# Expert blocks over chosen rows only, with the state space layer of one half of the tokens beneath the expert blocks of the other

## The chip, the cores and the metric

The program runs on one core of a Trainium2 chip. The metric is the device time of one execution in microseconds, the median of several runs. TensorE (PE in the profile) multiplies, VectorE (DVE) and ScalarE (ACT) work elementwise and read PSUM, GpSimd (POOL) works on SBUF only, and the queue of SyncE (SP) starts the transfers between memory and SBUF.

## What is computed

2048 tokens (8 sequences of 256) of width 256, all in float32, go through four layers, each added to its input and then normalised:

```python
x = layernorm(x + attention(x))      # 16 heads of 128, causal
x = layernorm(x + moe0(x))           # 32 experts of width 96, the 6 best of each token, plus a shared one of 192
x = layernorm(x + state_space(x))    # in-projection, 4-tap convolution, 8 heads, gate, out-projection
x = layernorm(x + moe1(x))           # 16 experts of width 176, the 4 best of each token, plus a shared one of 352
```

An expert is `silu(x @ gate) * (x @ up) @ down`, weighted per token by the router's normalised score; the weight of an expert that a token did not choose is zero.

## The kernel before

**Attention.** Eight groups of two heads (`group`) run over 16 units each (two heads by eight sequences). Each product of two float32 matrices is done as three passes over rounded halves (`hi` and `lo`, type float32r; helper `passes`, issued by `chain` at L352). Beside it ACT and POOL split the weights of the later layers into such halves, 56 items of 128x768 (`split_high` L650, `split_low` L544), and SP stores them to memory.

**Expert layers.** They are dense: every token goes through every expert. The hidden units of all experts and of the shared one are cut into tiles of 128. A step `s` is one hidden tile for one quarter (quad) of the tokens, 512 of them. `gate_up(s)` multiplies with the gate and the up weights: 2 outputs by 2 chunks by 3 passes, 12 matmuls of 512 columns. ACT takes the silu (`gate`, L742), DVE the product (`activate`, L1082), POOL multiplies with the router's weights, which a transfer has spread over the partitions (`combine`, L578), ACT and DVE round the result into halves (`high`, L750; `low_half`, L1088), and `down(s)`, two steps later, adds it to the output of the quad: 4 token tiles by 3 passes, 12 matmuls of 256 columns. There are 204 steps (4 quads by 26 tiles for the first expert layer, 4 by 25 for the second).

**State space layer.** A pair is 512 tokens (two sequences). The work of pair `p` is written out by hand beneath the steps, at offsets from `FRONT = 33, 65, 97, 129`: ten in-projections (`project`), the convolution (`conv_start`, `taps`, `conv_silu`), a scan of decays over 128x768 for each head (`decays` L1152), its product with the Gram matrix on POOL (`mixes` L600), the head's product on PE (`products`), outputs (`outputs` L1160 and L1163), the out-projection (`project_out`), and `out_add` L1181. `ln_stats`, `ln_root` and `ln_rows` (L920 to L934) normalise a quad.

The order on each engine is the order in which the program issues. An engine never goes past an instruction that waits. SP also waits in its order, for buffers that come free. After the last step DVE adds the last quad (`add_down`), normalises it and SP stores it (L488).

Of the kernel before, what the change touches and what calls it, by code (L numbers as in the profile page):

```python
# [7 lines left out]
I32 = mybir.dt.int32  # L8
# [32 lines left out]
L0 = dict(layer=0, experts=32, width=96, shared=192, top=6, rows=32, reuse=3)  # L41
L1 = dict(layer=1, experts=16, width=176, shared=352, top=4, groups=4, top_groups=2, rows=16, reuse=11)
LAYERS = L0, L1
for _l in LAYERS:
    _l["lead"] = -(-_l["shared"] // P)
    _l["tiles"] = _l["lead"] + _l["experts"] * _l["width"] // P
    _l["combs"] = _l["experts"] * _l["rows"] // P
# [8 lines left out]

IN_JOBS = 10
PART = 256
IN_ITEM = L0["tiles"]
L1_ITEM = IN_ITEM + -(-IN_JOBS // 3)  # L60
SPLITS = 8
ITEMS = SPLITS * (GROUPS - 1)
assert L1_ITEM + L1["tiles"] <= ITEMS

STEPS = QUADS * (L0["tiles"] + L1["tiles"])
LAG = 2
HALF = P // 2


def step(s):  # L70

    n = QUADS * L0["tiles"]
    if s < n:
        return L0, s // L0["tiles"], s % L0["tiles"]
    return L1, (s - n) // L1["tiles"], (s - n) % L1["tiles"]


def first_step(f, q):
    return f["layer"] * QUADS * L0["tiles"] + q * f["tiles"]


def shared(s):
    f, _, j = step(s)
    return j < f["lead"]


def packed(s):

    f, _, j = step(s)
    return f["shared"] % P == HALF and j == f["shared"] // P  # L90


def ups(s):

    return sum(not packed(i) for i in range(s + 1))


def rows_of(s):

    return slice(HALF, P) if packed(s) else slice(0, P)  # L100


def combed(s):

    return sum(not shared(i) for i in range(s + 1))


def comb_blocks():

    for f in LAYERS:  # L110
        for q in range(QUADS):
            for m in range(f["combs"]):
                s0 = first_step(f, q) + f["lead"] + m * f["reuse"]
                yield f, q, m, s0, s0 + f["reuse"] - 1


COMBS = list(comb_blocks())


def comb_block(s):  # L120
    f, q, j = step(s)
    return f["layer"] * QUADS * L0["combs"] + q * f["combs"] + (j - f["lead"]) // f["reuse"]


def comb_landed(k):

    return sum(16 * (P // COMBS[i][0]["rows"]) for i in range(k % 2, k + 1, 2))


FRONT = 33, 65, 97, 129  # L130
NORM0 = None, 1, 10, 19
NORM1 = 28, 54, 82, 115


def program(nc, x_rows, x_cols, attn_w, l0_gate, l1_gate, w_all, ssm_cols, out_w, out):
    with ExitStack() as ctx:
# [36 lines left out]
        causal_at = keep.at  # L173
        causal = keep("causal", [P, 2 * P])
        x = keep("x", [P, TILES, D])
        xT_hi = keep("xT_hi", [P, DC, T], F32R)
        xT_lo = keep("xT_lo", [P, DC, T], F32R)
# [60 lines left out]
        def unit(u):  # L238
# [3 lines left out]


        TOP = 34 * 1024
        top_at = (nc.sbuf_usable_end - TOP) // 64 * 64
        assert r.at <= top_at
        low = Region(keep.at)
        gated, act_sb = low("gated", [P, 2, BANK]), low("act_sb", [P, 2, BANK])
        act_hi, act_lo = low("act_hi", [P, 2, BANK], F32R), low("act_lo", [P, 2, BANK], F32R)

        stage = Region(top_at)
        raw_stage = stage("raw_stage", [P, 2, 3 * PART])
        split_stage = stage("split_stage", [P, 2, 3, 2, PART], F32R)
        high = Region(top_at)
        GU_RING, D_RING = 3, 3
        gu_w = high("gu_w", [P, GU_RING, 2, 2, PART], F32R)
        d_w = high("d_w", [P, D_RING, 2, PART], F32R)
        high.at = max(high.at, stage.at)
        comb = high("comb", [P, 2, BANK])
        gate_w = [{n: high(f"l{i}_gate_{n}", [P, DC * f["experts"]], dt) for n, dt in (("raw", F32), ("hi", F32R), ("lo", F32R))}  # L260
                  for i, f in enumerate(LAYERS)]
        logit, score, weight, comb_tok = (high(n, [P, QUAD, 32]) for n in ("logit", "score", "weight", "comb_tok"))
        choices = [high(f"l{i}_choice", [P, QUAD, f["experts"] + 8]) for i, f in enumerate(LAYERS)]
        chosen = high("chosen", [P, QUAD, SEL])
        top8, group_top8 = high("top8", [P, QUAD, 8]), high("group_top8", [P, QUAD, 8])
        group_choice, group_chosen = high("group_choice", [P, QUAD, 16]), high("group_chosen", [P, QUAD, 16])
        row_stat = high("row_stat", [P, QUAD])
        combT, logitT = high("combT", [32, BANK]), high("logitT", [32, BANK])

        small = Region(causal_at)  # L270
        cols = small("cols", [P, CJ * (TAPS + 1) + 2 * EJ + 2])
        ones_col, a_col = small("ones_col", [P, 1]), small("a_col", [P, 1])
        dt_tok = small("dt_tok", [P, 4, NH])
        mean_sq, rms, rms_tmp = (small(n, [P, 4]) for n in ("mean_sq", "rms", "rms_tmp"))

        IN_RING, DECAY_RING, MIXES = 3, 2, 3
        in_w = low("in_w", [P, IN_RING, 2, PART], F32R)
        mix_hi, mix_lo = low("mix_hi", [P, 2, SEQ], F32R), low("mix_lo", [P, 2, SEQ], F32R)
# [1434 lines left out]
```

## Time and profile before

| | |
|---|---|
| median of 3 runs | 1664.05 us (1663.39 to 1666.93) |
| span of the profiled execution | 1664.1 us |
| busy PE / DVE / ACT / POOL | 1607.4 / 1131.1 / 764.6 / 628.7 us |
| moved by transfers | 277.75 MB |

The profiled execution's own time and its span are the same to 0.1 us, and both are those of the median. Busy times are sums over one engine's instructions. The duration of a matmul in the trace overlaps the one before it, so that a PE that is always busy need not be at its peak: the rate is read from the distance between the starts of neighbours.

### The profile page before, as it was taken

Reading aid. Unit: us, or ns where it says so; the run is one execution under the profiler, and the core shown is the slowest. Engines: PE = TensorE matmul, PEld = TensorE weight load, DVE = VectorE, ACT = ScalarE, POOL = GpSimd, SP = SyncE. Lnnn points to the kernel's source line nnn. Section 1 sums busy time; section 2 is a strip of 40 time slices with the busy share of each in tenths; the row PEclk is TensorE's granted clock in tenths of the full one; section 3 lists DMA queues with packets and bytes.
Section 4 is the critical chain, followed back from the end, with each engine's and each line's share of the span. In section 5 each row is a group of like instructions: output and inputs, shape, how many; then the busy total and the mean of one; then the engine's idle time right before and its main releaser. Section 6 shows DMA issues by size and latency. Waiting matters only on the chain.

```text
span 1664.1 us, 29632 instructions
## 1 busy us (share of the span) xinstructions
PE 1607.4 (97%) x9944; PEld 1403.7 (84%) x9944; DVE 1131.1 (68%) x2877; ACT 764.6 (46%) x1889; POOL 628.7 (38%) x379
## 2 busy tenths in 40 slices
PE   7999999999999979999999999999999999999997
PEld 6988888898888868888888888888888888888886
DVE  5878878787887765556467568748784867753533
ACT  5666656666665543434433443325333533323221
POOL 2322223232222004323377335841575147533242
PEclk9999999999999999999999999999999999999999
DMA  6444335343443016666676556655655466555563
GB/s 212 159 140 143 141 118 180 132 158 139 142 141 137 1 59 205 191 196 205 199 225 188 184 176 209 194 187 165 207 189 175 146 206 197 178 175 172 195 206 107
DMA packets 101241, 277.75 MB, mean 167 GB/s; under 512 B 13488, under 2 KB 17584, under 8 KB 100112
## 3 DMA queue, kind: packets, MB, share of 16 engines
q1 hardware_dynamic: 101136, 276.39, 51.6%
q8 instruction: 61, 1.00, 0.2%
q14 instruction: 44, 0.36, 0.1%
HBM read 229.18 MB, written 46.63 MB: 166 GB/s over the span
## 4 chain that ended last, share of the span: by engine, by line
PE 60%; issue 14%; DVE 13%; POOL 6%; ACT 4%; DMA 1%; SPq 1%; POOLq 0%; DVEq 0%; ACTq 0%
PE psum L352 54%; POOL act_sb L578 4%; PE psum L1324 2%; DVE s_sb L1019 1%; PE psum L1335 1%; PE psum L1514 1%; POOL mix L600 1%; ACT p_sb L701 1%; PE psum L1314 1%; ACT kT_hi L660 1%; DVE s_sb L1017 1%; DVE kT_lo L913 1%; DVE pT_lo L1034 1%; DVE x L934 1%; DVE p_sb L1027 1%
## 5 line engine op out<-in xcount | busy, mean ns | idle before, releaser
L352 PE MATMUL psum<-xT_hi,gu_w 128*128 128x512 f32 x1616 | 550.3, 401 | 4.2 <-DVE act_sb L1082 4.0
L578 POOL TENSOR_TENSOR act_sb<-act_sb,comb 128x512 f32<-128x512 f32 x184 | 311.1, 1691 | 614.8 <-DVE act_sb L1082 614.6
L1082 DVE TENSOR_TENSOR act_sb<-psum,gated 128x512 f32<-128x512 f32 x204 | 140.7, 690 | 378.9 <-PE psum L352 372.6
L742 ACT ACTIVATE gated<-psum 128x512 f32<-128x512 f32 x204 | 122.2, 599 | 600.3 <-PE psum L352 597.8
L352 PEld LDWEIGHTS psum<-xT_hi,gu_w 128*128 128x128 f32 x1616 | 304.2, 188 | 78.0 <-DVE act_sb L1082 5.6
L352 PE MATMUL psum<-xT_lo,gu_w 128*128 128x512 f32 x808 | 319.6, 395 | 0.0
L352 PEld LDWEIGHTS psum<-d_w,act_hi 128*128 128x128 f32 x1632 | 221.5, 188 | 19.7 <-issue 2.1
L544 POOL TENSOR_TENSOR split_stage<-raw_stage,split_stage 128x768 fp32r<-128x768 f32 x56 | 103.1, 1840 | 354.2 <-ACT split_stage L650 354.2
L352 PE MATMUL psum<-d_w,act_hi 128*128 128x256 f32 x1632 | 227.7, 282 | 0.4 <-ACT act_hi L750 0.4
L352 PEld LDWEIGHTS psum<-xT_lo,gu_w 128*128 128x128 f32 x808 | 152.2, 188 | 28.8
L1088 DVE TENSOR_TENSOR act_lo<-act_sb,act_hi 128x512 fp32r<-128x512 f32 x204 | 148.8, 729 | 2.1 <-ACT act_hi L750 1.8
L750 ACT ACTIVATE act_hi<-act_sb 128x512 fp32r<-128x512 f32 x204 | 127.3, 624 | 17.1 <-POOL act_sb L578 16.9
L699 ACT ACTIVATE p_sb<-s_sb,neg_max 128x128 f32<-128x128 f32 x128 | 51.5, 403 | 172.0 <-DVE neg_max L1019 172.0
L352 PE MATMUL psum<-d_w,act_lo 128*128 128x256 f32 x816 | 130.1, 282 | 0.0
L352 PE MATMUL psum<-xT_hi,aw_hi 128*128 128x512 f32 x256 | 104.1, 407 | 9.9 <-POOL aw_lo L540 9.9
L352 PEld LDWEIGHTS psum<-d_w,act_lo 128*128 128x128 f32 x816 | 111.2, 188 | 0.0
L352 PE MATMUL psum<-xT_hi,aw_lo 128*128 128x512 f32 x256 | 102.1, 399 | 0.0
L352 PE MATMUL psum<-xT_lo,aw_hi 128*128 128x512 f32 x256 | 101.8, 398 | 0.0
L600 POOL TENSOR_TENSOR mix<-mix,gram 128x768 f32<-128x768 f32 x32 | 94.3, 2947 | 0.0
L1026 DVE TENSOR_SCALAR p_sb<-p_sb,row_inv 128x128 f32<-128x128 f32 x128 | 83.1, 649 | 4.6
L352 PE MATMUL psum<-aw_hi,xT_hi 128*128 128x256 f32 x256 | 74.7, 292 | 9.7 <-DVE kT_lo L913 8.3
L352 PE MATMUL psum<-aw_hi,zT_hi 128*128 128x256 f32 x256 | 80.5, 315 | 2.5 <-DVE zT_lo L1039 2.5
(203 smaller groups left out, 3473.6 us busy)
## 6 DMA issues: line engine op xcount, KB each, us to landing
gu_w<-w_split SPq DMA_DIRECT2D x204, 512.0 KB, 3.6
d_w<-w_split SPq DMA_DIRECT2D x204, 256.0 KB, 3.8
w_split<-split_stage SPq DMA_DIRECT2D x56, 768.0 KB, 3.9
raw_stage<-w_all SPq DMA_DIRECT2D x56, 384.0 KB, 4.3
decay_all<-decay_dram SPq DMA_DIRECT2D x32, 384.0 KB, 5.3
in_w<-w_split SPq DMA_DIRECT2D x40, 256.0 KB, 4.1
aw_raw<-attn_w SPq DMA_DIRECT2D x8, 1024.0 KB, 6.3
comb<-l_comb_dram SPq DMA_DIRECT2D x128, 64.0 KB, 3.1
```

Of the source, the lines that this page charges most:

```text
L352: last = nc.tensor.matmul(out_ap, w, m, start=start and n == 0, stop=stop and n == len(pairs) - 1, **kw)
L544: pool.tensor_tensor(split_stage[:, k % 2, :, 1, :], raw_stage[:, k % 2, :].rearrange("p (j w) -> p j w", j=3), split_stage[:, k % 2, :, 0 ...
L578: pool.tensor_tensor(act_sb[:, s % 2, :], act_sb[:, s % 2, :], comb[:, comb_block(s) % 2, :], ALU.mult).then_inc(comb_done, 1)
L600: pool.tensor_tensor(mix[:, g % MIXES], mix[:, g % MIXES], gram[:], ALU.mult).then_inc(mix_ready, 1)
L660: act.activation(kT_hi[:, bp % 2, j // 2, :], bank, ACT.Copy).then_inc(qkv_hi, 1)
L699: act.activation(p_sb[:, u % 3, 0:P], s_sb[:, u % 2, 0:P], ACT.Exp, bias=neg_max[:, u % 3, 0:1], scale=-1.0, accum_out=row_sum[:, u % 3, 0:1])
L742: act.activation(gated[to, s % 2, :], psum[0:to.stop - to.start, G_BANK, :], ACT.Silu).then_inc(gated_ready, 1)
L750: act.activation(act_hi[rows_of(s), s % 2, :], act_sb[rows_of(s), s % 2, :], ACT.Copy).then_inc(act_hi_ready, 1)
L1026: dve.tensor_scalar(p_sb[:, u % 3, 0:P], p_sb[:, u % 3, 0:P], row_inv[:, u % 3, 0:1], None, ALU.mult)
L1082: dve.tensor_tensor(act_sb[r, s % 2, :], psum[r, G_BANK if packed(s) else U_BANK, :], gated[r, s % 2, :], ALU.mult).then_inc(t_ready, 1)
L1088: dve.tensor_tensor(act_lo[r, s % 2, :], act_sb[r, s % 2, :], act_hi[r, s % 2, :].bitcast(F32), ALU.subtract).then_inc(act_lo_ready, 1)
L1324: last = pe.transpose(psum[:, PT_BANK, i * P:(i + 1) * P], p_sb[:, u % 3, i * P:(i + 1) * P], ident[:])
```

## The change

**Expert layers.** The router's choice is turned into row numbers. For each half of the tokens (1024) every expert gets a region of 1024 rows in a scratch array `xs` in memory; `rank` counts on PE, with a triangular matrix, the place of each token in each chosen expert's region, `slots` turns it into row numbers, and POOL scatters each token row there (`scatter`: one indirect transfer of 128 rows of 1 KB per token tile and choice). `table` works out which regions hold how many blocks of 128 rows. The stream of blocks is then of fixed length: per half 79 blocks in the first expert layer and 47 in the second, which is enough for any choice; what is left over works on rows of zeros. For each block SP reads the expert's number and row into registers, loads its weights (128x640 float32 in the first layer, 128x1280 in the second) and its rows (`block_load`), PE turns the rows, multiplies gate, up and down in plain float32 without halves, ACT copies and takes the silu, DVE multiplies, and SP stores two blocks of output at once (`block_store`). For each token tile POOL gathers the 6 or 4 output rows of each token back (`gather`, one indirect transfer for each choice), and DVE adds them with their weights (`combine`). The shared experts are 32 more blocks in each layer, with weights that stay in SBUF. `xs` is zeroed in memory during the attention, 77 MB in 42 transfers from SP, in place of the splitting of weights.

**Order.** Stream: 32 shared blocks of layer 0; 79 blocks of its half 0; 79 of its half 1; 16 shared and 47 of layer 1, half 0; 16 shared and 47 of layer 1, half 1. The combining of layer 0, the state space layer and the routing of layer 1 for half 0 are placed in 90 slots beneath the 79 blocks of layer 0, half 1; those of half 1 in 90 slots beneath the 63 blocks of layer 1, half 0. The state space layer multiplies in plain float32 as well, with in-projection weights that stay in SBUF, and the roundings into halves go. The attention's own code is the same, but three quads instead of one are normalised and two routed in its last group.

The core of the diff:

```diff
+HALVES = 2
+BLOCK = 128
+STREAM = shared_blocks(L0, range(TILES))
+FIRST = {}
+for _f, _h in ((L0, 0), (L0, 1), (L1, 0), (L1, 1)):
+    if _f is L1:
+        FIRST["shared", _h] = len(STREAM)
+        STREAM += shared_blocks(L1, range(HALF_TILES * _h, HALF_TILES * (_h + 1)))
+    FIRST[_f["layer"], _h] = len(STREAM)
+    STREAM += routed_blocks(_f, _h)
+FRONT = 8, 40
+SLOTS = 90
+SPAN = (FIRST[0, 1], FIRST["shared", 0]), (FIRST["shared", 0], FIRST["shared", 1])
+def mix_slot(j):
+    return 1 + j if j < QUAD else 16 + 4 * (j - QUAD)
+def gather_slot(j):
+    return max(0, mix_slot(j) - (1 if j < QUAD else 3))
...
+            def scatter(f, q):
+                if f["layer"] == 0 and q == 0:
+                    pool.wait_ge(xs_zeroed, 16 * ZEROED * (GROUPS - 1))
+                pool.wait_ge(placed, QUADS * f["layer"] + q + 1)
+                for t in range(QUAD * q, QUAD * (q + 1)):
+                    for k in range(f["top"]):
+                        pool.indirect_dma_start(xs[q // 2], bass.IndirectOffsetOnAxis(ap=row_of[:, t, k:k + 1], axis=0), x[:, t, :], None) \
+                            .then_inc(scattered[q], 16)
...
+                for k in range(f["top"]):
+                    pool.indirect_dma_start(og[:, i % MIX_RING, k, :], None, os[f["layer"]][t // HALF_TILES],
+                                            bass.IndirectOffsetOnAxis(ap=back_of[f["layer"]][:, t, k:k + 1], axis=0)).then_inc(og_loaded[i % MIX_RING], 16)
...
+            def block_gate_up(n):
+                for i in range(3 if f["layer"] else 2):
+                    at = i * h.stop
+                    last = chain(psum[h, gu_bank(n), i * P:(i + 1) * P], [(w[:, c * f["up"] + at:c * f["up"] + at + h.stop], rows[c]) for c in range(DC)])
+                last.then_inc(gu_ready, 1)
+            for n in range(BLOCKS):
+                if n + 2 < BLOCKS and is_routed(n + 2):
+                    block_turn(n + 2)
+                if n + 1 < BLOCKS:
+                    block_gate_up(n + 1)
+                block_down(n)
...
+            def combine(f, t):
+                dve.wait_ge(b_copied, OUTPUTS[SHARED_AT[f["layer"], t] + SHARED])
+                chained(dve.tensor_tensor(x[:, t, :], x[:, t, :], acc[:, t, :], ALU.add))
+                dve.wait_ge(og_loaded[i % MIX_RING], 16 * gathered(f, t))
+                for k in range(f["top"]):
+                    ins = dve.scalar_tensor_tensor(x[:, t, :], og[:, i % MIX_RING, k, :], mix_of[f["layer"]][:, t, k:k + 1], x[:, t, :], ALU.mult, ALU.add)
...
             def project(p, k):
-                n, part = IN_JOBS * p + k, slice(p * PT, (p + 1) * PT)
-                pe.wait_ge(in_loaded[n % IN_RING], 16 * (n // IN_RING) + 16)
-                pairs = []
-                for c in range(DC):
-                    w = slice(c * P, (c + 1) * P)
-                    pairs += passes(in_w[:, n % IN_RING, 0, w], in_w[:, n % IN_RING, 1, w], xT_hi[:, c, part], xT_lo[:, c, part])
-                chain(psum[:, proj_bank(k), :], pairs).then_inc(proj_ready, 1)
+                part = slice(p * PT, (p + 1) * PT)
+                chain(psum[:, proj_bank(k), :], [(in_w[:, k, c, :], xT[:, c, part]) for c in range(DC)]).then_inc(proj_ready, 1)
...
+                        if o == 48:
+                            scatter(L1, p)
...
+            all_stored(L1, 1)
+            for t in range(HALF_TILES, TILES):
+                gather(L1, t)
```

## Rows read from the trace of the kernel before

**Rows 1.** The page, busy us (share) xinstructions; and the group that counts the steps

```profile
PE 1607.4 (97%) x9944; PEld 1403.7 (84%) x9944; DVE 1131.1 (68%) x2877; ACT 764.6 (46%) x1889; POOL 628.7 (38%) x379
L1082 DVE TENSOR_TENSOR act_sb<-psum,gated 128x512 f32<-128x512 f32 x204 | 140.7, 690 | 378.9 <-PE psum L352 372.6
```

**Rows 2.** Windows: attention, expert steps, tail (PE, PEld, DVE, ACT, POOL, clock, DMA)

```profile
0.00:611.00 611.00, 571.63 (x3990) 517.53 (x3991) 479.51 (x1586) 378.84 (x1251) 146.44 (x103) 1.00 0.38 132
611.00:1654.00 1043.00, 1035.75 (x5956) 886.17 (x5954) 645.40 (x1266) 385.80 (x638) 482.30 (x276) 1.00 0.60 188
1654.00:1664.00 10.00, 0.00 (x0) 0.00 (x0) 6.19 (x26) 0.00 (x0) 0.00 (x0) 0.70 0.15 52
```

**Rows 3.** Timeline of PE, float32r matmuls of one expert step

```profile
830.46 0.63 PE L352 MATMUL psum<-xT_hi,gu_w 128*128 128x512 f32 x2
830.93 0.39 PE L352 MATMUL psum<-xT_lo,gu_w 128*128 128x512 f32 x1
...
831.39 1.11 PE L352 MATMUL psum<-d_w,act_hi 128*128 128x256 f32 x8
832.33 0.64 PE L352 MATMUL psum<-d_w,act_lo 128*128 128x256 f32 x4
832.80 0.39 PE L352 MATMUL psum<-xT_hi,gu_w 128*128 128x512 f32 x1
```

**Rows 4.** Timeline of PE, plain float32: transposes, then matmuls of 256, 256, 128, 128

```profile
823.50 0.60 PE L1495 MATMUL psum<-ident,conv 128*128 128x128 f32 x4
823.86 0.48 PE L352 MATMUL psum<-xT_hi,gu_w 128*128 128x512 f32 x1
```

```profile
803.77 0.92 PE L1484 MATMUL psum<-later,conv 64*128 64x256 f32 x4
804.62 0.50 PE L352 MATMUL psum<-xT_hi,gu_w 128*128 128x512 f32 x1
```

**Rows 5.** Groups of DVE and ACT by form: busy us, mean ns of one

```profile
L1152 DVE TENSOR_TENSOR_SCAN mix<-decay_all,start_row 128x768 f32<-128x768 f32 x32 | 82.5, 2579 | 0.1
L1181 DVE SCALAR_TENSOR_TENSOR x<-psum,rms,x 128x256 f32<-128x256 f32 x16 | 7.0, 476 | 0.0
L1143 DVE TENSOR_TENSOR h_tok<-psum,dt_tok 128x512 f32<-128x512 f32 x16 | 10.9, 682 | 0.0
L713 ACT ACTIVATE zT_hi<-psum 128x256 fp32r<-128x256 f32 x128 | 49.7, 388 | 2.2 <-PE psum L1335 1.4
L708 ACT ACTIVATE pT_last<-psum 128x128 f32<-128x128 f32 x128 | 33.9, 265 | 3.5 <-PE psum L1324 3.5
```

**Rows 6.** POOL's products and SP's issue of a transfer: ns min/median/max, or mean

```profile
L600 POOL TENSOR_TENSOR mix<-mix,gram x32: 1832/3294/3307, 834.0 to 1433.3; 128x768 f32<-128x768 f32 x32
L484 SPq DMA_DIRECT2D decay_all<-decay_dram x32: 377/431/674, 809.5 to 1412.8; - x32
```

```profile
L578 POOL TENSOR_TENSOR act_sb<-act_sb,comb 128x512 f32<-128x512 f32 x184 | 311.1, 1691 | 614.8 <-DVE act_sb L1082 614.6
```

**Rows 7.** Attention: one DVE line (ns min/median/max), then waits (us, times, longest)

```profile
L1026 DVE TENSOR_SCALAR p_sb<-p_sb,row_inv x128: 285/289/1561, 28.3 to 601.4; 128x128 f32<-128x128 f32 x128
```

```profile
PE psum L1324 <- DVE pT_lo L1034: 14.0, 18, 2.4
PE psum L352 <- DVE kT_lo L913: 8.3, 9, 2.0
```

**Rows 8.** Timeline of DVE and SP after the last matmul

```profile
1653.77 1.29 DVE L1095 TENSOR_TENSOR x<-psum,x 128x512 f32<-128x512 f32 x2 [1.12 <-PE psum L352]
...
1659.33 1.38 DVE L934 TENSOR_SCALAR x<-x,mv,rstd 128x256 f32<-128x256 f32 x4
```

```profile
1660.74 0.39 SPq L488 DMA_DIRECT2D out<-x  x1
```

More of the change, by code:

```diff
@@ L57 @@
 IN_JOBS = 10
[L58 to L84, printed above, removed]
@@ L87, in packed @@
[L87 to L114, printed above, removed]
@@ L117, with shared_blocks @@
[L117 to L135, printed above, removed]
+def shared_blocks(f, tiles):
+    return [(f, None, t, s) for t in tiles for s in range(SHARED)]
@@ new lines, with is_routed, gives_output @@
+SHARED_AT = {(f["layer"], t): n for n, (f, h, t, s) in enumerate(STREAM) if h is None and s == 0}
+def is_routed(n):
+    return STREAM[n][1] is not None
+def gives_output(n):
+    return is_routed(n) or STREAM[n][3] == SHARED - 1
+ROUTED = [n for n in range(BLOCKS) if is_routed(n)]
+ROUTED_OF = {n: r for r, n in enumerate(ROUTED)}
+OUTPUTS = [0]
+for _n in range(BLOCKS):
+    OUTPUTS.append(OUTPUTS[-1] + gives_output(_n))
+L0_ROUTED = HALVES * L0["blocks"]
+XB_RING, OUT_RING = 4, 4
+L1_RING = 4
@@ new lines, with out_place, ring_of, gathered @@
+L0_RING = 2 * L1_RING
+def out_place(n):
+    f, h, m, _ = STREAM[n]
+    before = sum(-(-STREAM[FIRST[k]][0]["blocks"] // 2) for k in ((0, 0), (0, 1), (1, 0), (1, 1)) if FIRST[k] < FIRST[f["layer"], h])
+    return before + m // 2, m % 2
+def ring_of(r):
+    if r < L0_ROUTED:
+        return r % L0_RING, r // L0_RING
+    r -= L0_ROUTED
+    k = r % L1_RING
+    return k, len(range(k, L0_ROUTED, L0_RING)) + r // L1_RING
+def gathered(f, t):
+    return sum(LAYERS[i]["top"] for i in range(2) for u in range(TILES)
+               if (i, u) <= (f["layer"], t) and (i * TILES + u) % 2 == (f["layer"] * TILES + t) % 2)
@@ L271, in program @@
[L271 to L278, printed above, removed]
-        square, square_sum = low("square", [P, PT]), low("square_sum", [P, PT])
@@ new lines, in _, with first_row_of @@
+            rows_of = {}
+            def first_row_of(n):
+                f, h, m, _ = STREAM[n]
+                if m % 8 == 0:
+                    if m == 0:
+                        sp.wait_ge(rows_known, HALVES * f["layer"] + h + 1)
+                    _, rows_of[f["layer"], h] = nc.values_load_multi_w_load_instructions(
+                        rows_at[f["layer"]][h][0:1, m:m + 8], engines=[mybir.EngineType.SP], min_val=0, max_val=f["last_row"],
+                        skip_runtime_bounds_check_because="a sum over all experts of rows that exist, whoever chose what")
+                return rows_of[f["layer"], h][m % 8]
@@ L521, in _ @@
                         store(q)
-            store(QUADS - 1)
+            for q in range(2, QUADS):
+                store(q)
             sp.wait_ge(stored, 16 * QUADS)
@@ new lines, in weights @@
+                of = by_expert(place, f)[:, tiles, :]
+                chained(dve.scalar_tensor_tensor(of, of, 1.0, shift[:, h, 0:e].rearrange("p (a e) -> p a e", a=1).to_broadcast([P, QUAD, e]),
+                                                 ALU.add, ALU.add))
+                chained(dve.tensor_tensor(of, of, by_expert(mask, f)[:, tiles, :], ALU.mult))
+                for i in range(QUAD):
+                    last = dve.max(places[:, QUAD * q + i, :], of[:, i, :])
+                chained(last)
```

1405 lines of the change are left out of this document (707 added, 698 removed).

## Prediction

> **What bounds the kernel now.** I read the page first, then windows by stage, then PE's timeline inside an expert step, then the groups of the other engines, and the end. The page gives PE 97% of the span [rows 1]. The windows cut this into attention to 611 us, 204 expert steps from 611 to 1654, and a tail of 10 us [rows 2]. In the expert stage PE is busy 1035.75 of 1043 us at full clock, DVE 645, POOL 482, ACT 386, with the transfer engines at 0.60 [rows 2]. PE's order alone sets this stage: 5.1 us a step. Inside it the starts give the rates. Two float32r matmuls of 512 columns take 0.47 us (0.235 each), twelve of 256 columns 1.41 us (0.118 each) [rows 3]. A step is 12 of each, 4.23 us, so 863 us for 204; the other 180 us are the state space layer and the normalisations beneath. The reader should see that the change must be judged on PE first, and then on whoever becomes late once PE is relieved.
>
> **Prices on PE in plain float32.** A plain float32 product shows in the trace as two instructions. The four of L1484 (256, 256, 128 and 128 columns) take 0.85 us to the next start [rows 4]. Two passes over 768 columns at the rate of [rows 3] would be 0.71; four would be 1.41 and one 0.35, so it is two an instruction, and the 0.14 left goes with the change to another type. So I take 0.235 us per instruction of 256 columns and 0.118 per one of 128: four times the float32r price per column, against three passes before. A transpose of 128 costs 0.09 [rows 4], taken as 0.10. A block of layer 0 is then 2 transposes (0.20), 4 products of 128 columns (0.94) and one of 256 (0.47): 1.61 us. A block of layer 1 is 0.20 + 6 x 0.235 + 2 x 0.47 = 2.55 us. Shared blocks have no transposes: 1.41 and 2.35 us.
>
> The sum of the blocks on PE: 158 x 1.61 = 254, 94 x 2.55 = 240, 32 x 1.41 = 45, 32 x 2.35 = 75, together 614 us for 863: 249 us less. The state space layer gets dearer. For each of four pairs: 10 in-projections of 2 x 0.94 (was 6 x 0.235), 18.8 us; 8 heads of 1.41, 11.3 us; 16 out-products of 0.47, 7.5 us; turns, Gram products and routing about 6. That is 43.6 a pair, 87 for a half.
>
> **Stage by stage**, with what else binds there.
>
> *Attention, 605 us (was 611).* The 56 splits go from ACT and POOL. They also held up DVE: L1026 takes 289 ns in the median and up to 1561 [rows 7]. But PE waits for DVE here only 22 us in all [rows 7], and the last group gets two more normalisations and one more routing on DVE, about 15 us of which half shows. Bounds 595 to 620.
>
> *32 shared blocks, 60 us.* PE 45 plus 5 for turns and routing. DVE has about 28 us of routing and normalising among the first 12 blocks, where PE has 22, so 10 us are lost.
>
> *79 blocks of layer 0, half 0, 155 us.* PE needs 127. Each block moves 328 KB of weights, 131 KB of rows in and 131 KB out, 46.6 MB in all, and 48 scatters add 6.3 MB. The window of the expert stage moves 188 GB/s at a share of 0.60 [rows 2], which would be 313 GB/s when full: 169 us. Short packets may cost more, long ones less; at 370 GB/s it is 143. I take 155: transfers bind here for the first time.
>
> *POOL's indirect transfers.* There are 96 + 64 scatters and as many gathers, 320 in all. The trace of before has none. Nearest rows: SP's issue of a transfer, 0.43 us, and a POOL product of 128x512, 1.69 us [rows 6]. I take 1.0 us, about the middle, and keep 0.43 and 1.7. The trace shows no transfer started by POOL. The Trainium skill (DMA: Bandwidth & Descriptors, "Latency and other measured facts") gives about 1 us to the first byte of a transfer that GpSimd prepares; by it the sum would be the same, and no run here shows it yet.
>
> *79 blocks of layer 0, half 1, over the state space layer of half 0, 269 us.* PE 127 + 87 + 2 = 216. DVE: 79 products (0.27, as ACT's 128x128 from PSUM [rows 5]) 21; 8 combines of 7 chained operations of 256 columns, 0.48 each [rows 5], 28; four normalisations of a quad, 5.6 each (first to last row of the tail, less the add [rows 8]), 22; state space 90, of it 16 scans of 2.58 [rows 5]; routing and out_add 29. That is 190 in 216. ACT: 79 x (0.39 + 0.27 + 0.39) = 83 [rows 5], plus 66. So no engine is over PE in sum, but PE, DVE and POOL wait for each other in order. (1) At the start, slots 0 to 3 gather four tiles: 4 for the stores to land, 24 on POOL, 2 to land, 3.5 for the last combine, against 5.6 us in which PE reaches slot 4 and 3 of slack: 25 lost. DVE stands at the combine, block products are queued behind it, and PE waits for them. (2) In slots 13 to 28 POOL has four gathers (24) and eight products of 2.95 (23.6; mean of 3.29 and less [rows 6]) in 42 us of PE: 5. (3) At slot 56 the 16 scatters of pair 0 (16 us) stand before the products of pair 1, which have 5 to 8 us of lead: 11. (4) DVE's bursts, a normalisation or a routing of 5 us, against a lead of about 4 us: 12. Sum 269.
>
> *63 blocks of layer 1, half 0, over half 1, 296 us.* PE 38 + 120 + 87 = 245. The start is worse, since the scatters of pair 1 were issued two slots before the end: 31. Then 3, 9 and 8 for the other three.
>
> *63 blocks of layer 1, half 1, 175 us.* PE 158. The 47 routed ones move 43 MB and the gathers 4 MB, at 313 to 370 GB/s 150 to 127 us, after 38 us of shared blocks that move little: 165 to 188. I take 175, with transfers as the bound again.
>
> *Tail, 49 us (was 10).* After the last store (3), 32 gathers at 1.0, 2.5 to land, a last combine 2.5, one normalisation 5.6, the store 3.3 (1660.74 to the end [rows 8]). Nothing covers this.
>
> Sum: 605 + 60 + 155 + 269 + 296 + 175 + 49 = 1609, say **1610 us**. The sum stands against the profiled execution's 1664.1 us, which is the median of the runs: 3.3% faster. PE's own need from the first block to the last falls from 1036 us to 50 + 127 + 216 + 245 + 158 = 796, so 240 us are gained there and 199 given back: 160 as waits, 104 of them in the two overlapped stages, and 39 in the tail.
>
> **Rivals.**
>
> *A. The waits are hidden, PE sets the end.* For it: DVE has 190 of 216 us, and before PE lost only 7 of 1043 us to anyone [rows 2] with a DVE at 62%. Against it: blocks are three times shorter than steps, so the same burst is no longer covered. With indirect transfers at 0.5 us and half of my waits: 600 + 52 + 143 + 235 + 262 + 162 + 35 = 1490 us.
>
> *B. POOL is slower: the kernel ends slower.* Place: the gathers at the start of both overlapped stages, the scatters at slot 56, the tail. My sum holds 150 exposed indirect transfers (24 + 40 + 2 x 16 + 32, and some 20 at slots 13 to 28). Each 0.1 us more costs 15 us, so above 1.36 us the change loses. A POOL product rises from 1.83 to 3.29 us when DVE scans beside it [rows 6]. If the transfers cost as L578's product, 1.69, the sum is 1610 + 104 = 1714 us. The Trainium skill (SBUF - State Buffer, "Who interferes with whom") says that GpSimd and a DVE operation with two SBUF inputs or a two-port mode take one port in turn, and that descriptors wait for it as well; L600's two durations agree. That rule speaks against this change, and this is its rival.
>
> *C. Transfers bind.* Rows of 1 KB are new to this trace. At 250 GB/s half 0 of layer 0 takes 53 MB / 0.25 = 212 us and the last stage 38 + 188 = 226, the two between keep 252 and 240 under what they need anyway: 1610 + 57 + 51 = 1718 us. For it: 0.6 busy already at 188 GB/s [rows 2]. Against: nearly every packet before was 2 KB or more and so are the weights.
>
> *D. The hand-over inside a block binds:* PE to ACT to DVE to PE for 128 columns, 0.27 + 0.27 and two semaphores, under 1.16 us of PE. If 0.3 us of it shows in each of 316 blocks, plus 95: 1705 us.
>
> **Chances.** Forecast (1560 to 1655) 0.37; A 0.24; B 0.24; C 0.06; D 0.06; in between and within 0.2% of before 0.03. 0.2% (3 us) is about what a measurement of this kernel can tell from no change. Forecast and A are faster, 0.61; B, C and D are slower, 0.36. The range 1490 to 1720 leaves out the far halves of A and B. The likeliest case's own range is 1560 to 1655.
>
> **What would show it.** Right: PE's starts 0.118 us apart in blocks; DMA share near 1 from 665 to 820 us; DVE idle before `combine` for POOL or its transfers at the start of both overlapped stages; POOL idle little in slots 13 to 28; 40 us without a matmul at the end. Wrong: an indirect transfer of 0.5 or of 1.7 us on POOL; PE idle in small pieces in every block (D); PE idle for weights or rows (C).

## The result, and the profile after

The changed kernel takes **1994.5 us** (1992.6 to 1995.9, four runs) against 1663.8 us: 1.198 times as long (95% interval 1.196 to 1.199). Forecast was 1610, with 1490 to 1720 as the range: wrong in size and in sign.

Timed again unchanged, on three further occasions, it took 1847.7, 1844.7 and 1992.3 us, while the kernel before, run beside it each time, stayed at 1664.9 to 1665.7. So it has **two levels**, about 1846 and 1993, one per occasion: none of its 16 executions lay between, and one chip showed both (the high one with the changed kernel, the low one at another time with two close variants). I call them the low and the high level. The first profile is of the high one. The error has two parts that must be kept apart: 236 us that are always there, and 147 that come with the high level.

The page after, answering to [rows 1]: busy times, then PE, POOL and PE's granted clock in 40 slices of 50 us.

```profile
PE 1511.0 (76%) x9344; PEld 1256.6 (63%) x9344; DVE 975.6 (49%) x3299; ACT 759.6 (38%) x2327; POOL 442.1 (22%) x422
...
PE   7999999999973418788457977827898787877760
...
POOL 1010100000006470000515134261511503122015
PEclk9999999999986658799779988868998897888885
```

PE is no longer the bound (97% before). Where POOL's slice is high, PE's is low: 600 to 750, 950 to 1000, 1300 to 1350 us. The windows by stage, for [rows 2]: attention, the shared blocks as far as they are held up (614 to 754 us), the rest of them, 79 blocks of layer 0 half 0, 79 over the state space layer of half 0, 63 of layer 1 over half 1, the last 63, the tail. Columns: PE, PEld, DVE, ACT, POOL, clock, DMA share, GB/s.

```profile
0.00:614.00 614.00, 576.31 (x4018) 527.34 (x4019) 444.06 (x1654) 335.05 (x1193) 53.52 (x60) 0.98 0.42 155
614.00:754.00 140.00, 35.28 (x186) 31.27 (x184) 20.63 (x110) 8.95 (x25) 85.36 (x95) 0.57 0.29 98
754.00:787.00 33.00, 32.07 (x223) 29.40 (x224) 9.21 (x37) 13.78 (x38) 0.00 (x0) 0.90 0.06 18
787.00:956.00 169.00, 136.69 (x945) 117.15 (x944) 44.49 (x163) 77.55 (x237) 0.00 (x0) 0.94 0.84 269
956.00:1286.00 330.00, 237.24 (x1366) 188.19 (x1366) 157.64 (x435) 127.48 (x310) 109.95 (x89) 0.86 0.59 183
1286.00:1666.00 380.00, 290.62 (x1521) 212.03 (x1521) 184.90 (x495) 123.75 (x301) 119.04 (x103) 0.86 0.50 160
1666.00:1934.00 268.00, 202.75 (x1092) 151.20 (x1091) 85.74 (x321) 72.95 (x227) 42.89 (x45) 0.87 0.59 188
1934.00:1994.00 60.00, 0.00 (x0) 0.00 (x0) 28.88 (x87) 0.09 (x1) 31.32 (x32) 0.51 0.30 90
```

From 614 to 754 us PE works 35 of 140 us, DVE 21 and ACT 9. The groups of the operations that I had to price, for [rows 5, 6]:

```profile
L633 POOL DMA_INDIRECT og<-l_os,l_back_of x160 | 161.4, 1009 | 575.0 <-DMA l_os<-b_out 310.1
...
L618 POOL DMA_INDIRECT xs<-x,row_of x160 | 159.9, 1000 | 236.3 <-DVE row_of L1026 189.4
```

The timelines of ACT and of SP in the stop. In brackets: the idle time before, and what ended it.

```profile
690.49 0.27 ACT L790 ACTIVATE b_gated<-psum 96x128 f32<-96x128 f32 x1 [1.31 <-PE psum L407]
708.27 0.27 ACT L790 ACTIVATE b_gated<-psum 96x128 f32<-96x128 f32 x1 [17.51 <-remote]
713.22 0.39 ACT L803 ACTIVATE acc<-psum 128x256 f32<-128x256 f32 x1 [4.68 <-remote]
734.98 0.27 ACT L790 ACTIVATE b_gated<-psum 96x128 f32<-96x128 f32 x1 [21.37 <-remote]
753.20 0.27 ACT L790 ACTIVATE b_gated<-psum 96x128 f32<-96x128 f32 x1 [17.94 <-remote]
```

```profile
717.40 0.72 SPq L511 DMA_DIRECT2D xb<-xs  x1
720.93 0.71 SPq L505 DMA_DIRECT2D bw<-l_w  x1
```

The product of PE that ACT waits for at 708.27 had ended at 696.6. "Remote" says that the profile finds no work which ended then: the update of the semaphore itself came 11.7 us late. SP needs 0.7 us for an issue (0.33 without such a string), and the trace's records of its register operations between two issues show 0.70 for most of them (0.03 to 0.07 otherwise). DVE, whose steps release one another, kept its pace inside the stop: L1019 to L1026 start at 708.79, 709.10, 709.42 and 709.93 us, with the same spacing as at 683.84 before that string. All ended at 753 us, 7 us after POOL's last scatter. The end, for [rows 8], DVE's last row and SP's store:

```profile
1989.42 1.38 DVE L954 TENSOR_SCALAR x<-x,mv,rstd 128x256 f32<-128x256 f32 x4
1990.83 0.38 SPq L541 DMA_DIRECT2D out<-x  x1
```

The attention's waits are as small as foretold: PE's waits for DVE answer to [rows 7] with 7.9 and 6.8 us (14.0 and 8.3).

```profile
PE psum L1401 <- DVE pT_lo L1138: 7.9, 11, 2.9
PE psum L407 <- DVE kT_lo L933: 6.8, 9, 0.8
```

### The profile page after: what moved, and what is told of

Read it like the earlier page. It is cut to its first block, busy times and chain, and to the rows that moved or that the text cites. A ratio compares the mean times of both kernels' runs of the same rounds, so it can differ in the third digit from the quotient of the medians.

```text
span 1994.2 us, 30357 instructions
## 1 busy us (share of the span) xinstructions
PE 1511.0 (76%) x9344; PEld 1256.6 (63%) x9344; DVE 975.6 (49%) x3299; ACT 759.6 (38%) x2327; POOL 442.1 (22%) x422
## 4 chain that ended last, share of the span: by engine, by line
PE 45%; DVE 15%; issue 10%; DMA 8%; another core or an unknown queue 8%; ACT 7%; POOL 4%; SPq 2%; DVEq 0%; ACTq 0%; POOLq 0%
PE psum L407 37%; DMA xb<-xs 8%; PE psum L1579 2%; POOL xs L618 2%; POOL og L633 2%; PE psum L1401 1%; ACT p_sb L730 1%; DVE x L1095 1%; PE psum L1550 1%; SPq L505 1%; DVE s_sb L1123 1%; PE psum L1412 1%; DVE stats L940 1%; ACT p_sb L728 1%
## 5 line engine op out<-in xcount | busy, mean ns | idle before, releaser
L407 PE MATMUL psum<-xbT,bw 128*96 128x128 f32 (+1 forms) x2392 | 338.6, 293 | 0.0
L407 PEld LDWEIGHTS psum<-xbT,bw 128*96 128x96 f32 (+1 forms) x2392 | 312.8, 194 | 0.6 <-issue 0.3
L633 POOL DMA_INDIRECT og<-l_os,l_back_of x160 | 161.4, 1009 | 575.0 <-DMA l_os<-b_out 310.1
L407 PE MATMUL psum<-bw,b_act 96*128 96x256 f32 (+2 forms) x692 | 229.1, 424 | 63.9 <-ACT b_out L803 20.0
L618 POOL DMA_INDIRECT xs<-x,row_of x160 | 159.9, 1000 | 236.3 <-DVE row_of L1026 189.4
L779 ACT ACTIVATE xbT<-psum 128x256 f32<-128x256 f32 x252 | 96.3, 382 | 249.1 <-PE psum L1579 230.1
L407 PEld LDWEIGHTS psum<-bw,b_act 96*128 96x128 f32 (+2 forms) x692 | 113.6, 206 | 103.5 <-issue 75.9
L1579 PE MATMUL psum<-ident,xb 128*128 128x128 f32 x504 | 110.2, 302 | 75.6 <-DMA xb<-xs 71.1
L803 ACT ACTIVATE b_out<-psum 128x256 f32<-128x256 f32 x252 | 96.8, 384 | 130.7 <-PE psum L407 125.8
L407 PE MATMUL psum<-xT,l_shared_w 128*128 128x128 f32 (+1 forms) x640 | 102.2, 317 | 0.0
```

Of the source, the lines that this page charges most:

```text
L407: last = nc.tensor.matmul(out_ap, w, m, start=start and n == 0, stop=stop and n == len(pairs) - 1, **kw)
L618: pool.indirect_dma_start(xs[q // 2], bass.IndirectOffsetOnAxis(ap=row_of[:, t, k:k + 1], axis=0), x[:, t, :], None) \
L633: pool.indirect_dma_start(og[:, i % MIX_RING, k, :], None, os[f["layer"]][t // HALF_TILES], bass.IndirectOffsetOnAxis(ap=back_of[f["layer" ...
L779: act.activation(xbT[:, r % 2].rearrange("p c t -> p (c t)"), psum[:, TURN_BANK, 0:DC * BLOCK], ACT.Copy).then_inc(xbT_ready, 1)
L803: act.activation(to, psum[:, DOWN_BANK, 0:D], ACT.Copy).then_inc(b_copied, 1)
L1579: last = pe.transpose(psum[:, TURN_BANK, c * BLOCK:(c + 1) * BLOCK], xb[:, r % XB_RING, c * P:(c + 1) * P], ident[:])
```

## Experiments

Twelve different kernels in eighteen runs, each with the kernel before beside it. Ratios are to that kernel. Diffs are cut to the edit.

**few** and **plain**: fewer indirect transfers, or plain ones.

```diff
# few: scatter and gather alike
-for k in range(f["top"]):
+for k in range(1):
# plain: scatter (gather alike)
-pool.indirect_dma_start(xs[q // 2], IndirectOffsetOnAxis(ap=row_of[:, t, k:k + 1], axis=0), x[:, t, :], None)
+pool.dma_start(xs[q // 2][at:at + P], x[:, t, :])
```

> The changed kernel with one indirect transfer per tile and layer in place of six or four: 32 scatters and 32 gathers, where 320 were; the other chosen rows are neither laid out nor brought back (the sums take the first one again), so the output is not the reference's. Theory S (a string of indirect transfers on POOL holds up the other engines: the updates of semaphores by PE arrive 9 to 18 us late and SP takes 0.7 us for a register operation): the 32 shared blocks take 60 to 80 us in place of some 170, the starts of both overlapped stages lose their stops of 30 to 60 us, and the time is 1700 to 1760 us. Rival T (the engines wait only for POOL's own time, 1.27 us a transfer): 256 transfers fewer, of which I had some 150 exposed, 190 us less, of which none in the shared blocks: they still take about 170 us and the time is 1800 to 1850.

> The changed kernel with all 320 indirect transfers of POOL replaced by plain ones of the same size, in the same places, with fixed rows: the output is not the reference's. If any string of transfers that POOL prepares holds up the other engines, PE still does almost nothing in the stretch from 614 to 754 us (35 us of 140) and the time is within 40 us of 1994. If it is the indirect form (reading offsets, one descriptor a row) that does it, the shared blocks take 60 to 80 us and the time is 1750 to 1850, less still if a plain transfer occupies POOL for less than the 0.96 us of an indirect one.

few: 1741.7 us, ratio 1.045 (1.038 to 1.051). plain: 1767.2, ratio 1.060 (1.056 to 1.063). In both, the shared blocks end at 682 us, where they ended at 787. That spoke for theory S and for the indirect form, and both times fell into its ranges; but xbfirst, timed on the same occasion, had all its indirect scatters and ended the shared blocks at 680 as well. So the numbers came out by luck: the occasion was one of the low level, where nothing is held up, and neither theory was tested. Against the low level few gains 106 us for 256 transfers fewer. plain gains 80 us (76 beside the changed kernel itself, in plain2), and its transfers occupy POOL for less:

```profile
L618 POOL DMA_DIRECT2D xs<-x x160 | 86.5, 549 | 177.5 <-DVE row_of L1025 177.0 <-issue 0.5
```

An indirect one takes 0.95 to 1.0 us and leaves POOL idle another 0.30 behind it, 1.27 in a string. So 320 x 0.72 = 230 us less of POOL gave 76 to 80, a third of a microsecond for one. I had 150 of 320 transfers exposed, 0.47. Note that even at 0.55 us a transfer the change loses 100 us: the price of the indirect form does not decide the sign.

**xbfirst** and **l1first**: SP asks for a block's rows before it waits for the place of its weights; in both layers, or in layer 1 alone.

```diff
-                sp.wait_ge(b_down_done, ...)
-                sp.dma_start(bw[...], expert_w[...]).then_inc(bw_loaded[k], 16)
                 wait(sp, xb_turned, r - XB_RING + 1)
                 sp.dma_start(xb[...], xs[h][bass.ds(row, BLOCK)]).then_inc(xb_loaded[r % XB_RING], 16)
+                sp.wait_ge(b_down_done, ...)
+                sp.dma_start(bw[...], expert_w[...]).then_inc(bw_loaded[k], 16)
```

> The changed kernel with one edit: SP issues the load of a block's rows before it waits for the block that frees the weights' place, and the weights after. Theory L (in layer 1 the rows are asked for only one block of PE, 2.6 us, before they are turned, and land later than that): the 47 routed blocks of the last stage take 3.3 to 3.6 us each in place of 4.26 (200 us from 1734 to 1934), the same in part in layer 1's half 0, and the time falls by 40 to 70 us to 1925 to 1955. Rival: the transfers' volume or the hand-over PE, ACT, DVE, PE inside a block binds there; the last stage stays at 4.1 to 4.3 us a block and the time within 10 us of 1994. If the weights then come late in place of the rows, the gain is under 15 us and PE waits for weights.

> Rows before weights in layer 1 alone; layer 0's loads as in the changed kernel. If the order of the loads in layer 0 has a part in the stop beneath the scatters, the stop is there as in the changed kernel: shared blocks end at about 786 us, the last stage takes 154 us in place of 200, and the time is 1910 to 1950. If the stop comes and goes with anything (chance, the place of the code), shared blocks may end at 680 us and the time is 1785 to 1850.

xbfirst: 1790.7 us, ratio 1.076 (1.072 to 1.079). l1first: 1798.1, ratio 1.080 (1.078 to 1.082), beside the changed kernel at 1847.7 (**again**, ratio 1.110, 1.108 to 1.112): 50 us for an exchange of two issues. The last 47 blocks, first of again, then of l1first, as windows and then as waits (us in total, times, longest):

```profile
1579.00:1784.00 205.00, 157.79 (x831) 118.24 (x830) 65.34 (x230) 60.71 (x185) 22.72 (x24) 0.86 0.67 216
```

```profile
1584.00:1736.00 152.00, 133.10 (x830) 100.31 (x829) 65.12 (x230) 59.90 (x184) 22.69 (x24) 0.98 0.87 289
```

```profile
PEld psum L1579 <- DMA xb<-xs: 59.6, 33, 3.3
```

```profile
PEld psum L1588 <- DMA xb<-xs: 25.2, 25, 3.2
```

205 us became 152, and PE's clock in it rose from 0.86 to 0.98. Theory L is shown. (The total of xbfirst, foretold as 1925 to 1955, belongs to the low level and not to the theory.) In layer 1 over the state space layer the same edit gave 3 us (366 to 363): there a block takes longer and rows come in time.

> The changed kernel itself, unchanged, beside the next three. With rows first, the same 96 scatters stood back to back and the shared blocks took 61 us in place of 114 from the first to the last, with not one late semaphore. If the stop of the other engines beneath the scatters belongs to the program, the time is again 1990 to 2000 with gaps of 15 to 35 us between 611 and 754 us. If it belongs to the chip or to chance, the time here is 1830 to 1900 and the gaps are absent or elsewhere.

**spaced**: an addition on POOL over 128x512 behind each scatter of layer 0.

> The changed kernel with a POOL addition over 128x512 (about 1.3 us) behind each of the 96 scatters of layer 0, so that they come about 2.6 us apart in place of 1.27. Theory S, with density as the cause: PE runs the shared blocks beneath them nearly freely (over 60 us busy within the 100 us after the first scatter, where 35 of 140 were), the routed blocks of half 0 start when quads 0 and 1 are laid out, about 125 us after 603, and the time is 1930 to 1980. If each transfer costs the others a fixed stop whatever the distance, or POOL's own time is all that counts, the string is twice as long, half 0 starts at 800 us or later and the time is 2010 to 2110.

1910.8 us, ratio 1.147 (1.142 to 1.153): dearer than the changed kernel at the low level, whose string it doubled. So it tested nothing of theory S: there was no stop to cure, but two costs. The rows of half 0 were laid out at 716 us in place of 664, and the blocks waited (shared blocks end at 725). And DVE's operations with two SBUF inputs slowed under the additions; the same two groups in spaced, then in again (604 to 800 us):

```profile
L1071 DVE TENSOR_TENSOR weight<-weight,row_stat 128x128 f32<-128x128 f32 x4 | 6.3, 1572 | 0.1
L1067 DVE TENSOR_TENSOR weight<-mask,score 128x128 f32<-128x128 f32 x4 | 5.4, 1354 | 0.0
```

```profile
L1063 DVE TENSOR_TENSOR weight<-mask,score 128x128 f32<-128x128 f32 x4 | 1.2, 294 | 0.0
L1067 DVE TENSOR_TENSOR weight<-weight,row_stat 128x128 f32<-128x128 f32 x4 | 1.2, 291 | 0.1
```

0.29 us became 1.35 to 1.57, and the four bursts of routing weights stopped PE for 8 us each in place of at most 4. This is the exclusive port of the Trainium skill ("SBUF — State Buffer", "Who interferes with whom"), and the trace agrees. The scatters of again, which lie beneath the same operations, leave them at 0.29.

**late**: the first scatter waits for two shared blocks.

> The changed kernel with the first scatter held until PE has finished two shared blocks, so that no scatter lies beneath the last units of the attention. If the stop arises where the scatters begin beneath the attention, the shared blocks run at 1.4 to 2 us each under them, the routed blocks start when quads 0 and 1 are laid out, at about 690 us, and the time is 1880 to 1920. If any string beneath any work stops the others, the stop is only moved and the time is 1990 to 2010.

1860.6 us, ratio 1.116 (1.114 to 1.118), at the low level, where no stop was there to be moved. It says only that the scatters, begun 21 us later (at 624.6), cost 13 us: the routed blocks wait for them.

**spread**: on xbfirst, the scatters of layer 1 four at a time, behind the products of their slot.

```diff
-                        if o == 48:
-                            scatter(L1, p)
+                        for j in range(QUAD):
+                            if o == 48 + (3 * j if i == 0 else j // 2):
+                                scatter_tile(L1, p, QUAD * p + j)
```

> Rows first, and the 16 scatters of layer 1 per quad, which stood in one string before the products of POOL that PE waits for, are issued four at a time, three slots apart, behind the products of their slot. My terms (3) were 11 and 9 us; the gaps of PE at slot 56 measured 16.0 and 12.4 us in rows first. If the scatters before the products are their cause, both gaps go and the time falls by 20 to 30 us to 1760 to 1770. If something else made PE wait there, the gaps stay and so does 1790.

1761.7 us, ratio 1.058 (1.055 to 1.061). The gaps of 16.0 and 12.4 us are gone, and 29 us with them (against xbfirst, timed on another occasion). My term (3) had the right place and cause and two thirds of the size.

**shift**: on spread, the state space layer 27 slots later, so that blocks cover the first gathers.

```diff
-FRONT = 8, 40
-SLOTS = 90
+FRONT = 35, 67
+SLOTS = 117
-    return 1 + j if j < QUAD else 16 + 4 * (j - QUAD)
+    return (12, 18, 25, 32)[j] if j < QUAD else 38 + 4 * (j - QUAD)
```

> Built on spread (rows first, scatters of layer 1 spread; 1761.7 us): the state space layer starts 27 slots later in a span of 117 slots in place of 90, the first four gathers are awaited at slots 12, 18, 25 and 32 in place of 1 to 4, and the second quad's scatters of layer 1 follow the first gathers of the next span. My term (1), the stop at the start of both spans (25 and 31 us foretold, 32 and some 40 read), should be covered by blocks: 1690 to 1725 us. If the stop is not POOL's string but the end of the stores or the DVE, it moves with the slots and the time stays within 15 us of 1762.

1736.9 us, ratio 1.043 (1.040 to 1.046). 25 us gained (against spread, timed on another occasion), less than I expected; the stops of 11, 6, 6 and 4 us at the start of the first span shrank to one of 10. Term (1) is real. This is the best version found, and still 4% slower than before.

**again2, plain2, loop**: the level again, and a string by itself beneath the attention.

```diff
                 low_part(g, 3)
+                if not isinstance(g, int):
+                    for k in range(24):
+                        pool.indirect_dma_start(junk[k], bass.IndirectOffsetOnAxis(ap=junk_row[:], axis=0), causal[:], None).then_inc(junk_done, 16)
+                    pool.wait_ge(junk_done, 16 * 24 * g)
```

> The changed kernel itself once more. It took 1994.5 us where it was first timed and 1847.7 us the second time, with the kernel before at 1663.8 and 1665.4 us in the same places. If there are two kinds of place, it is 1990 to 2000 or 1843 to 1852 here and nothing between; the three kernels beside it then say what the dear kind costs each of them.

> The same kernel as plain, 320 plain transfers from POOL in place of the indirect ones, beside the changed kernel in the same place. POOL was occupied 0.55 us by each, where an indirect one with the gap behind it takes 1.27. If the changed kernel takes 1848 here, this one takes 1755 to 1775. If the changed kernel takes 1994 here and only indirect transfers stop the others, it is 1755 to 1775 as well; if any transfer that POOL prepares does, it is over 1850.

> The changed kernel with 24 indirect scatters of a constant tile to spare memory in each of the attention groups 1 to 6, back to back, 30 us of every 75, and nothing else changed: the string by itself beneath other work. If a string holds up the other engines wherever it lies, the six groups lose 10 us or more each, 60 in all, against the changed kernel beside it. If it costs them nothing but POOL's own time, which is free there, the difference is under 10 us.

again2 1844.7 us, ratio 1.109 (1.106 to 1.111); plain2 1768.4, ratio 1.060 (1.055 to 1.064); loop 1857.1, ratio 1.114 (1.112 to 1.118). All at the low level, where 144 indirect transfers beneath the attention cost 12 us.

**again3, lighter**: the level, and half of the weights' bytes on top of shift.

> The changed kernel a third time beside the others. Two kinds of place: 1843 to 1852 or 1990 to 2000 us. If it is 1990 or more, the gaps of 15 to 35 us beneath the scatters of layer 0 are back, with semaphores of PE delivered 10 us and more late; if it is 1845, the first timing stays the only one of its kind and its cause open.

> Built on shift (1736.9 us): from the ninth routed block on only the first half of each block's weights is loaded, the other half stays what it was, so the output is not the reference's. Stages without the state space layer: half 0 of layer 0 took 160 us at 315 GB/s and the last 47 blocks 153 us at 287 GB/s. If transfers bind there, they fall to PE's own 130 to 140 and 125 to 135 us and the time is 1680 to 1700. If PE, its clock or the hand-over inside a block binds, they stay within 5 us and the time is 1725 to 1740.

again3 1992.3 us, ratio 1.198 (1.195 to 1.201): the high level. lighter met it too: 1887.0, ratio 1.132 (1.129 to 1.135), its shared blocks ending at 785 us, so its total says nothing of the bytes. Its two stages without the state space layer say more. They took 151 and 149 us (160 and 153 in shift) at 219 and 201 GB/s in place of 315 and 287:

```profile
786.00:937.00 151.00, 131.94 (x937) 117.54 (x935) 44.35 (x163) 74.77 (x236) 0.00 (x0) 0.93 0.73 219
1676.00:1825.00 149.00, 136.28 (x830) 102.30 (x828) 65.09 (x229) 59.62 (x184) 22.67 (x24) 0.95 0.67 201
```

So halving the weights is worth some 9 and 4 us. The comparison is across the levels: in shift 40 scatters still run beneath the first of the two stages, in lighter none. The changed kernel itself, with the same difference, took 167 and 169 us there, so the scatters do not explain the 9. In the first, PE is busy 132 of 151 us, and four waits of up to 3.8 us for DVE's bursts are 15 of the other 19. Neither of my cases held whole.

**plain0, loop2, then loop3, plain0b**: the same two kernels until each had met the high level. plain0 makes layer 0's scatters plain and leaves the others indirect.

> The changed kernel with the 96 scatters of layer 0 as plain transfers of POOL to fixed rows (output not the reference's); layer 1's scatters and all gathers stay indirect and show which kind of place it is. In the cheap kind: shared blocks end at about 680 us and the time is within 15 us of 1846. In the dear kind, if the indirect form does the harm: shared blocks end at 680 us still, while the later strings stop PE, and the time is 1870 to 1900. If any string of POOL's transfers does it, they end at 720 us or later.

> The same kernel as loop: 24 indirect scatters to spare memory beneath each of the attention groups 1 to 6, whose instructions repeat. In the cheap kind of place it was 12 us over the changed kernel. In the dear kind, if a string holds up the others wherever it lies, each group loses 10 to 25 us and the time is 2060 to 2140; if it needs code that runs once (instructions that must be fetched), the groups stay at 75 us and the time is 2000 to 2015.

> The kernel loop once more, to meet the dear kind of place. Its shared blocks show the kind: they end at about 680 us in the cheap one and 786 us in the dear one, and the time is about 1855 or above 1990. In the dear kind, groups 1 to 6 stay at 75 us each if code that runs once is needed for the stop, and take 85 us or more each if not.

> The kernel plain0 once more: layer 0's scatters plain, all others indirect. The later strings show the state: in the dear one PE stops 20 us at the start of layer 0's half 1 and the last 47 blocks take 208 us, in the cheap one 197 to 204. If the state is dear and the indirect form is needed, the shared blocks end at about 680 us and the time is 1870 to 1900; if any string of POOL's does it, they end at 720 us or later. If the state is cheap, 1850 to 1862 and the question stays open.

plain0 1857.8 us (ratio 1.115, 1.111 to 1.119) and loop2 1851.4 (1.111, 1.098 to 1.125) met the low level, on the chip that had shown the high one. loop3 met the high level: 2147.9 us (a single execution, 1667.3 beside it). The same 75 us of the attention in loop2, then in loop3:

```profile
300.00:375.00 75.00, 72.36 (x512) 65.86 (x511) 56.35 (x199) 43.28 (x158) 28.46 (x28) 1.00 0.54 203
```

```profile
300.00:375.00 75.00, 52.53 (x340) 47.67 (x339) 35.65 (x137) 29.47 (x107) 25.07 (x25) 0.82 0.52 198
```

(2147.9 - 1992.3) / 6, some 26 us, are lost per string of 24, and the groups of loop3 follow each other at 101 us in place of 75. This is beneath instructions that repeat: loading of code that runs once is not the cause. Nor is other loading of code: from 180 to 670 us, with five of the strings in it, loop3 moved data on these two queues and nothing on those that bring instructions.

```profile
q1 hardware_dynamic: 28080, 60.30, 33.4%
q0 software_dynamic: 5760, 15.74, 8.1%
```

plain0b met the high level: 1889.4 us, ratio 1.134 (1.117 to 1.151). Its later indirect strings stopped PE for up to 19.4 and 18.7 us at the two span starts (in plain0 up to 11.0 and 14.8). Its 96 plain scatters in a row did nothing to anyone, and its shared blocks ended at 681 us:

```profile
600.00:681.00 81.00, 64.88 (x460) 59.92 (x461) 42.05 (x205) 25.56 (x70) 54.17 (x103) 0.92 0.54 188
```

So the high level needs the indirect form. What switches it stays open: the changed kernel met both, one chip met both, and strings beneath the attention and behind it were held up alike. What else ran on the chip at the time was not recorded.

## Why the prediction was wrong, step by step

The changed kernel at the low level (again), windows as above; the stages are those of the prediction's sum, with the tail last:

```profile
614.00:681.00 67.00, 59.16 (x405) 54.34 (x404) 29.34 (x145) 22.28 (x60) 51.30 (x59) 0.90 0.40 137
681.00:848.00 167.00, 136.71 (x947) 116.07 (x945) 44.46 (x163) 77.67 (x237) 35.25 (x36) 0.95 0.92 303
848.00:1163.00 315.00, 238.21 (x1368) 188.05 (x1366) 165.03 (x435) 128.41 (x311) 109.61 (x89) 0.87 0.61 192
1163.00:1529.00 366.00, 288.51 (x1521) 209.73 (x1521) 186.66 (x494) 124.10 (x302) 122.44 (x104) 0.87 0.52 166
1529.00:1784.00 255.00, 202.14 (x1093) 151.00 (x1091) 85.86 (x322) 73.28 (x227) 41.89 (x44) 0.88 0.61 197
1784.00:1843.00 59.00, 0.00 (x0) 0.00 (x0) 28.88 (x87) 0.00 (x1) 31.22 (x32) 0.51 0.31 91
```

| stage | foretold | low level | high level |
|---|---|---|---|
| attention and 32 shared blocks | 665 | 681 | 787 |
| layer 0, half 0 | 155 | 167 | 169 |
| layer 0, half 1, over state space | 269 | 315 | 330 |
| layer 1, half 0, over state space | 296 | 366 | 380 |
| layer 1, half 1 | 175 | 255 | 268 |
| tail | 49 | 59 | 60 |

The low level exceeds the sum by 1843 - 1609 = 234 us. This splits into five parts: 37 us more work on PE, 92 of PE's work done at half clock, 86 more idle time of PE, 9 in the attention and 10 in the tail. To get the first two, I laid PE's busy time in the trace of again over the stretches in which the granted clock stood at its lower level (1.2 in place of 2.4 GHz), and took half of the busy time there as work, the other half as what the clock cost.

- **PE's work** was 37 us too low. Counted so, the five stages from 614 us on hold 52.6 + 128.6 + 218.1 + 262.1 + 171.7 = 833 us of work at full clock, against 796. At full clock a shared block of layer 0 takes 1.31 us (1.41 foretold), a routed one 1.6 (1.61); one of layer 1 takes 2.76 (2.55), 94 x 0.2 = 20 us more.
- **The clock was missing from the sum.** This is the step that failed most. I priced PE at full clock throughout, as [rows 2] have it. But an engine that waits in pieces was granted less, 0.87 in both spans, and then its work takes longer. In the same five stages PE is busy 925 us, 92 over the 833: 7, 8, 20, 26 and 30. The last 47 blocks show that this is the clock and not the work. They hold 129, 130 and 130 us of work in again, l1first and shift, done in 158, 133 and 134 us. So of the 53 us that l1first gains there, 25 are clock and 28 are idle time. In the other stages no run tells how much of the clock's share lies on the path.
- **The waits** were too small: PE idles 8, 30, 77, 77 and 53 us in the five stages, 245 in all, where I had 160. The two spans have 24 and 26 too many. The largest excess, 36 us, is in the last stage, and the next point has its cause.
- **The lead of layer 1's rows was missed.** I costed each transfer by its bytes, never by when SP may issue it. The rows of block n + 3 stand on SP behind the wait for block n - 1, one block of PE (2.6 us) before they are turned. It cost 50 us in the last stage, clock included, of the 80 by which that stage was wrong. I had put the 17 us over PE's need down to volume; lighter shows 4 for half of the weights.
- **The indirect transfer**: 1.0 us foretold, 0.96 measured, but 0.30 idle behind each makes it 1.27. The tail's 32 gathers explain 9 of its 10 us by this; over all, 0.27 x 320 / 3 = 29 us, an estimate from plain's slope. The Trainium skill's microsecond to the first byte ("DMA: Bandwidth & Descriptors", "Latency and other measured facts") is no price for POOL's occupation, and a plain one has 0.55.
- **The terms of the two spans.** (1) and (3) stood in the right places: (1) 32 and some 40 us idle for 25 and 31, (3) 16 and 11 for 11 and 9. (4), DVE's bursts, is 17 us of PE's waits from 905 to 1065 us for 12. (2), POOL's gathers and products, shows there as one wait of 1.3 us for 5.
- **Rival B** had the right side, in the main by luck: its point of loss was 1.36 us and the transfer took 1.27, so by its own reckoning the change should have won, and plain at 0.55 still loses. The clock and SP's order had already used up the gain. **C** is a small term, the transfers at 303 to 315 GB/s in layer 0 as assumed. (Its argument that nearly every packet before was 2 KB or more is true of the bytes and not of the count: 17584 of 101241 were smaller.) **D** does not show: in lighter's 79 blocks 4 of 151 us are left over for it. **A** is refuted: of the waits I listed all but (2) showed in full.
- **The high level** was in no rival. I asked what a string of transfers does to POOL's own queue, not what it does to the semaphores and to SP. It adds 147 us: 106 in the shared blocks, which I took to be free of POOL, the rest at the later strings. The Trainium skill holds that a DMA never contends with a compute engine ("SBUF — State Buffer", "Who interferes with whom"). At the low level the trace agrees: the shared blocks over 96 scatters ended at 681 us, as with plain ones. At the high one PE's semaphore updates and SP's operations are held up, 11.7 us and 0.7 us in the rows above. The rule speaks of SBUF's ports, and no run here shows by which path they are held up; the measurement decides.

## What to carry to other kernels

When an engine's load is cut, price its work at the clock that a waiting engine is granted, and follow every load back to the moment when its queue may issue it: a wait for one buffer in front of another buffer's load took a whole block of lead here. An indirect transfer was 1.3 us of GpSimd per 128 rows; put no other engine behind a string of them, keep strings short, and use plain transfers where rows are fixed. Time such a kernel on more than one occasion before believing any number.

## What the runs showed of the hardware

- Indirect transfer of 128 rows of 1 KB from POOL: 0.96 us and 0.30 us idle, scatter and gather alike; plain one 0.55 us, no gap.
- Two levels of one program, 8% apart, each steady within 0.6% on an occasion. In the high one a string of indirect transfers delays PE's semaphore updates by 10 to 20 us (the first late one beneath the 10th transfer of the first string, at 614.7 us), and SP's register operations take 0.7 us. A string of 96 plain ones did not (plain0b).
- DVE's 128x128 operation with two SBUF inputs: 0.29 us alone, 1.35 to 1.57 under POOL's 128x512 additions, 0.29 under indirect transfers.
- Plain float32: 0.11 us per instruction of 128 columns at full clock (0.118 foretold).
- PE's work in the last 47 blocks is 129 to 130 us in three runs; the granted clock made of it 158 us (0.86) or 133 (0.98).
